# A gated delta-rule layer with a ternary feed-forward: weight sums taken in the recurrence's last chunk, GpSimd's tables moved forward

## The reference

```
q, k, v = silu(causal_conv4(x @ Wq/Wk/Wv)); a = sigmoid(x @ Wa + ba); beta = sigmoid(x @ Wb + bb)
for t in 512 steps:                       # state St: 128 x 128 per batch and head
    err = St k_t - v_t
    St  = a_t * St - (beta_t * err) k_t^T
    o_t = St q_t
x = layernorm(x + ((norm(o) * ln_w + ln_b) * sigmoid(x @ Wg)) @ Wo)
```

```
scale = mean(|W|) + 1e-8
Wq    = clip(round(W / scale), -1, 1) * scale
x     = layernorm(x + (silu(x @ Wup^T) * (x @ Wgate^T)) @ Wdown^T)
```

## Time and profile before

| | |
|---|---|
| Time, median of 3 runs | 3029.47 us (3019.24 to 3034.47) |
| The profiled execution | 3027.24 us, of it the span of the profile 3025.5 us |
| Busy in the span | PE 2701.4, DVE 2054.5, POOL 1434.1, ACT 1184.1 us |
| Stages, from the windows of the trace | projections 0 to 935, recurrence 935 to 2222, attention output 2222 to 2551, ternary 2551 to 2624.6, feed-forward 2624.6 to 3025.5 us |
| Granted clock of TensorE (share of full speed) | recurrence 0.97, ternary 0.72 |
| GB/s in the ternary stage | 171 |

### The profile page before, as it was taken

One profiled execution on the slowest core, in us unless ns is written; L12 is line 12 of the kernel. 1 busy time (PEld: TensorE's weight loads), 2 busy tenths in 40 slices (PEclk: granted clock), 3 DMA queues, 4 the chain that ended last, 5 costly groups with the idle time before them and its releaser, 6 DMA issues. The chain is left out here.

```text
span 3025.5 us, 57383 instructions
## 1 busy us (share of the span) xinstructions
PE 2701.4 (89%) x18370; PEld 2279.9 (75%) x18370; DVE 2054.5 (68%) x5896; ACT 1184.1 (39%) x2305; POOL 1434.1 (47%) x1213
## 2 busy tenths in 40 slices
...
DMA packets 412562, 442.27 MB, mean 146 GB/s; under 512 B 122304, under 2 KB 367040, under 8 KB 389568
## 3 DMA queue, kind: packets, MB, share of 16 engines
...
...
## 5 line engine op out<-in xcount | busy, mean ns | idle before, releaser
L355 PE MATMUL pa_ps<-pa_x_hi,pa_w_hi 128*128 128x512 f32 x1296 | 507.5, 392 | 10.4 <-ACT pa_y L298 6.2
L355 PE MATMUL pa_ps<-pa_x_lo,pa_w_hi 128*128 128x512 f32 x1296 | 505.1, 390 | 0.0
L355 PE MATMUL pa_ps<-pa_x_hi,pa_w_lo 128*128 128x512 f32 x1296 | 504.9, 390 | 0.0
L1030 DVE TENSOR_TENSOR pb_tmp<-pb_gb,pb_ps 128x112 f32<-128x112 f32 (+6 forms) x1792 | 328.2, 220 | 98.7 <-POOL pb_gb L721 88.6
L438 DVE SCALAR_TENSOR_TENSOR pa_cv<-pa_y,pa_taps,pa_cv 128x2048 f32<-128x2048 f32 x144 | 354.8, 2464 | 17.8
L1035 DVE TENSOR_TENSOR pb_ps<-pb_ps,pb_tmp 128x112 f32<-128x112 f32 (+6 forms) x1792 | 331.3, 226 | 6.3 <-DVE pb_tmp L1030 3.1
L721 POOL TENSOR_TENSOR pb_gb<-pb_gb,pb_ng 128x448 f32<-128x448 f32 (+6 forms) x448 | 330.9, 778 | 2.3 <-DMA pb_gb<-scratch_pairs 2.3
L904 PEld LDWEIGHTS pb_ps<-pb_Gm,pb_XT 128*128 128x128 f32 x2048 | 248.7, 196 | 68.9 <-issue 38.6
L355 PEld LDWEIGHTS pa_ps<-pa_x_hi,pa_w_hi 128*128 128x128 f32 x1296 | 243.7, 188 | 69.0 <-ACT pa_y L298 11.1
L705 POOL TENSOR_TENSOR pb_UT<-pb_UT,pb_crow 128x1024 f32<-128x1024 f32 x120 | 280.5, 2361 | 11.9 <-DMA pb_crow<-scratch_crow 11.9
L355 PEld LDWEIGHTS pa_ps<-pa_x_hi,pa_w_lo 128*128 128x128 f32 x1296 | 243.7, 188 | 50.9
...
## 6 DMA issues: line engine op xcount, KB each, us to landing
...
```

The lines of the kernel that those rows point to most:

```text
L355: last = nc.tensor.matmul(out, w[:, mat, k, :], xx[:, k, b * S:(b + 1) * S], start=(k == 0 and n == 0), stop=(k == KT - 1 and n == 2))
L1030: tt(tmp[:, hs, 0:w], gb[n][:, hs, off[t]:off[t] + w], xs[:, qs, t:t + 1].broadcast_to([P, QUART, w]), ALU.mult).then_inc(s_mul, 1)
```

## The change

In `recurrence`, GpSimd's order within a chunk is another: `with_gates(c, 1)` stands directly behind `with_gates(c, 0)`, `with_gates(c, 2)` behind the first two decays, `with_gates(c, 3)` behind the scaling of slot (1, 0); decays 4 and 5 go between the scalings of block 1 and block 2. In the last chunk, SP loads the three feed-forward matrices in 12 pieces of 1 MB into the four free 1 MB areas of `kq[0]` and `crow`, and ScalarE takes from them 48 absolute sums over 512 columns, 6 after each slot's copies, into a tile `part` that outlives the stage. In `ternary`, the sums and ScalarE's part of them are gone; all three scales are made once, at the beginning; VectorE's two passes are `w * (1/scale) + M` with M = 1.5 * 2^23 (which rounds to a whole number) and a clamp to M-1 and M+1; ScalarE's copy out of PSUM subtracts M. The weights are still loaded a second time in `ternary`.

```diff
@@ recurrence, SP
+            def feed_forward_weights():
+                sp.wait_ge(s_tp, T_START + T_CH * (NCH - 2) + T_KT[3] + 1)
+                sp.wait_ge(s_dp, D_START + D_CH * (NCH - 1))
+                sp.wait_ge(s_us, 8 * (NCH - 1))
+                for k in range(PIECES):
+                    if k >= 4:
+                        sp.wait_ge(s_fa, 4 * (k - 3))
+                    sp.dma_start(ff_stage[k % 4].rearrange("p (n d) -> p n d", n=4),
+                                 weight_piece(ff_views, k // 4, k % 4)).then_inc(s_fw[k % 4], 16)
...
             chunk(NCH - 2, 0, True, False)
+            feed_forward_weights()
             chunk(NCH - 1, 1, False, False)
@@ recurrence, GpSimd
             def chunk(c, i, p, more):
                 with_gates(c, 0)
+                with_gates(c, 1)
...
+                with_gates(c, 2)
                 less_v(c, D_START + D_CH * c, 1)
-                with_gates(c, 1)
...
                         if (n, hf) == (1, 0):
-                            with_gates(c, 2)
-                        if (n, hf) == (1, 1):
                             with_gates(c, 3)
+                        if n + hf == 2 and more:
+                            if n == 1:
+                                pool.wait_ge(s_crl, 32 * c + 32)
+                                pool.wait_ge(s_dp, D_START + D_CH * c)
+                            decay(3 + n)
                 if more:
-                    pool.wait_ge(s_crl, 32 * c + 32)
-                    pool.wait_ge(s_dp, D_START + D_CH * c)
-                    for e in range(4, 8):
+                    for e in (6, 7):
                         decay(e)
@@ recurrence, ScalarE
+            def absolute(k):
+                j = k // 4
+                if k % 4 == 0:
+                    act.wait_ge(s_fw[j % 4], 16 * (j // 4 + 1))
+                piece = ff_stage[j % 4][:, 512 * (k % 4):512 * (k % 4) + 512]
+                nc.scalar.activation(piece, piece, ACT.Abs, accum_out=part[:, k // 16, k % 16:k % 16 + 1]).then_inc(s_fa, 1)
...
                         if not more:
+                            for k in range(6 * (2 * n + hf), 6 * (2 * n + hf) + 6):
+                                absolute(k)
                             continue
@@ ternary
-                nc.scalar.activation(junk[:, :, :], w[i % 2][:, 4 * j:4 * j + 4, :], ACT.Abs,
-                                     accum_out=part[:, i, j:j + 1]).then_inc(s_abs, 1)
...
-                    nc.scalar.activation(dest(tern, i, n), ps[2 + n % 4][:, :].rearrange("p (k e) -> p k e", k=4), ACT.Copy).then_inc(s_ev, 1)
+                    nc.scalar.activation(dest(tern, i, n), ps[2 + n % 4][:, :].rearrange("p (k e) -> p k e", k=4), ACT.Identity,
+                                         bias=back[:, 0:1]).then_inc(s_ev, 1)
...
+            nc.vector.tensor_reduce(tot[:, :], part[:, :, :], AX.X, ALU.add).then_inc(s_scale, 1)
+            nc.vector.tensor_scalar(scales[:, :], ps[0][:, 0:3], 1.0 / COUNT, 1e-8, ALU.mult, ALU.add).then_inc(s_scale, 1)
+            nc.vector.reciprocal(inv[:, :], scales[:, :]).then_inc(s_scale, 1)
...
-                    nc.vector.tensor_scalar(ll, ww, half[:, i, 1:2], None, ALU.is_lt).then_inc(s_low, 1)
-                    dve.wait_ge(s_low, 4 * i + j + 1)
-                    nc.vector.scalar_tensor_tensor(out=ww, in0=ww, scalar=half[:, i, 0:1], in1=ll, op0=ALU.is_gt, op1=ALU.subtract).then_inc(s_q, 1)
+                    dve.wait_ge(s_w[i % 2][j], 16 * (i // 2 + 1))
+                    nc.vector.tensor_scalar(ww, ww, inv[:, i:i + 1], MAGIC, ALU.mult, ALU.add).then_inc(s_q, 1)
+                    dve.wait_ge(s_q, 8 * i + 2 * j + 1)
+                    nc.vector.tensor_scalar(ww, ww, MAGIC + 1.0, MAGIC - 1.0, ALU.min, ALU.max).then_inc(s_q, 1)
```

More of the change, by code:

```diff
@@ L465, in _, with weight_views, weight_piece, recurrence @@
             head(NH - 1, False, False)
-def recurrence(nc, scr):
+def weight_views(mats):
+    return [mats[0].rearrange("(n p) d -> p n d", p=P), mats[1].rearrange("(n p) d -> p n d", p=P),
+            mats[2].rearrange("(n p) (m d) -> p n m d", p=P, d=HID)]
+def weight_piece(views, i, j):
+    return views[i][:, 4 * j:4 * j + 4, :] if i < 2 else views[i][:, j, :, :]
+def recurrence(nc, scr, mats, part):
     GR = HB // 4
@@ L541, in recurrence @@
         s_os = [m.sem(f"os{i}") for i in range(2)]
+        s_fw = [m.sem(f"fw{i}") for i in range(4)]
+        s_fa = m.sem("fa")
         T_START, T_CH = 12, 32
@@ L565, in recurrence @@
         flat = lambda t: t.rearrange("p h t -> p (h t)")
+        PIECES = 12
+        ff_views = weight_views(mats)
+        ff_stage = [flat(kq[0][:, 0, :, :]), flat(kq[0][:, 1, :, :]), flat(crow[:, 0:16, :]), flat(crow[:, 16:32, :])]
         window = lambda w: (slice(16 * w, 16 * w + 16), slice(max(16 * w - BL, 0), 16 * w + BL))
@@ L649, in _ @@
             sp.wait_ge(s_te, 8 + 4)
-            sp.dma_start(scr["crow"].rearrange("c h v -> h c v"), decay_rows).then_inc(s_cw, 16)
+            sp.dma_start(scr["crow"].rearrange("c h v -> h c v"), decay_rows).then_inc(s_cr, 16)
             load_kq(1, 1)
-            sp.wait_ge(s_cw, 16)
+            sp.wait_ge(s_cr, 32)
             load_crow(0, 0)
@@ L1430, in _, with ternary @@
                 nc.vector.bn_aggr(stat[:, c, :], bn_all[:, c, :])
-def ternary(nc, mats, tern, scales):
+def ternary(nc, mats, tern, scales, part):
     NP = E * HID // P // HID
     COUNT = float(E * HID)
+    MAGIC = 1.5 * 2.0 ** 23
     with ExitStack() as ctx:
@@ L1442, in ternary @@
         w = [m.sb(f"w{i}", [P, NP, HID]) for i in range(2)]
-        junk = m.sb("junk", [P, 4, HID], mybir.dt.bfloat16)
-        low = m.sb("low", [P, 4, HID])
         ident = m.sb("ident", [P, P])
         ones = m.sb("ones", [P, P])
-        part = m.sb("part", [P, 3, 4])
+        back = m.sb("back", [P, 1])
         tot = m.sb("tot", [P, 3])
-        half = m.sb("half", [P, 3, 2])
+        inv = m.sb("inv", [P, 3])
         ps = [m.ps(f"ps{i}") for i in range(8)]
         s_id = m.sem("id")
-        s_c = m.sem("c")
         s_w = [[m.sem(f"w{i}_{j}") for j in range(4)] for i in range(2)]
-        s_abs = m.sem("abs")
-        s_tot = m.sem("tot")
-        s_sum = m.sem("sum")
-        s_sc = m.sem("sc")
-        s_low = m.sem("low")
+        s_scale = m.sem("scale")
         s_q = m.sem("q")
@@ L1477, in _ @@
             make_identity(nc, pool, ident, s_id)
-            nc.gpsimd.memset(ones[:, :], 1.0).then_inc(s_c, 1)
+            nc.gpsimd.memset(ones[:, :], 1.0).then_inc(s_id, 1)
+            nc.gpsimd.memset(back[:, :], -MAGIC).then_inc(s_id, 1)
         @block.scalar
         def _(act):
-            def absolute(i, j):
-                act.wait_ge(s_w[i % 2][j], 16 * (i // 2 + 1))
-                if i or j:
-                    act.wait_ge(s_abs, 4 * i + j)
-                nc.scalar.activation(junk[:, :, :], w[i % 2][:, 4 * j:4 * j + 4, :], ACT.Abs,
-                                     accum_out=part[:, i, j:j + 1]).then_inc(s_abs, 1)
-            for i in range(2):
-                for j in range(4):
-                    absolute(i, j)
+            act.wait_ge(s_id, 4)
             for i in range(3):
@@ L1495, in _ @@
                     act.wait_ge(s_tr, NP * i + n + 1)
[L1496 to L1498 removed]
+                    nc.scalar.activation(dest(tern, i, n), ps[2 + n % 4][:, :].rearrange("p (k e) -> p k e", k=4), ACT.Identity,
+                                         bias=back[:, 0:1]).then_inc(s_ev, 1)
         @block.tensor
         def _(pe):
[L1502 to L1503 removed]
+            pe.wait_ge(s_id, 3)
+            pe.wait_ge(s_scale, 1)
+            nc.tensor.matmul(ps[0][:, 0:3], ones[:, :], tot[:, :], start=True, stop=True).then_inc(s_scale, 1)
             for i in range(3):
[L1505 to L1506 removed]
                 for n in range(NP):
                     j = NP * i + n
[L1509 removed]
+                    pe.wait_ge(s_q, 8 * i + 2 * (n // 4) + 2)
                     if j >= 4:
```

33 lines of the change are left out of this document (8 added, 25 removed).

## The result

The changed kernel takes 3015.86 us (median of 20 runs, 3002.19 to 3026.81), the kernel before in the same rounds 3038.99 (20 runs, 3019.24 to 3056.22): ratio 0.9922, 95% interval 0.9907 to 0.9937, so 23.7 us less (19 to 28). The direction is as predicted, the time is not: 2997.0 was said, 2982 to 3010 the range. The profiled execution took 3009.76 us, its span is 3008.0: 17.5 us less than the profiled one before.

A forecast was written before the change was run, and what follows sets the result against it. The TensorE-ScalarE ring was taken to bound the recurrence, VectorE its last chunk. From 3027.24 us, -3.3 - 4.2 + 8.5 - 32.4 = -31.4 gave 2995.8, with 2.2 for the median 2998; 2997 was said, range 2982 to 3010.

The forecast's parts named there:

- Ternary, -32.4: Ternary stage: two VectorE passes a piece fit under the 2.71 us DMA, so DMA bounds it; 32.4 us less.
- Rival D: Ternary stage: VectorE's two passes run at 2.35 us each, 25 us later, 3022; chance 0.05.
- Rival B: Ternary stage: TensorE stays at the low clock throughout, 10 us later, 3007; chance 0.11.
- The 48 sums, +8.5: Last chunk: ScalarE's sums at 0.62 us delay the copies of X, +7.4, plus 1.1 for TensorE's clock.
- 1.1 for one or two such slots: Last chunk: added for eight transposes at TensorE's low clock, 0.8 us a slot.
- Rival C: Last chunk: sums cost the upper bound, +17 (0.75 us each, every slot at low clock), 3006; chance 0.10.
- Chunk 0, -4.2: Chunk 0: table 1 made before GpSimd's wait for `crow`, so slot (1, 0)'s transposes start 4.2 us earlier; bounds 0 and 11.8.
- Chunks 1 to 14, -3.3: Tables moved forward end VectorE's wait; ScalarE's key copy is late next: 0.39 us in 7 chunks, 0.08 in 7.
- The reading of the ring: Recurrence: TensorE and ScalarE (transposes, copy, products, key copies, next copy of X) bound it; VectorE's 57.2 us wait lies beside.
- rival A: Recurrence: GpSimd's tables are on the path after all, 57.2 us go instead of 3.3, 2943; chance 0.05.
- Rival E: Recurrence: decay 4 waits for `crow` ahead of block 2's scaling, 3049; chance 0.03; sign: GpSimd waiting ahead of L732.
- the level: Whole kernel: starting time, the profiled execution's 3027.24 us, with the median of the runs put 2.2 us higher.

The follow-up runs named there:

- experiment 3: Changed kernel plus matmuls that nobody reads (fillers) on TensorE ahead of the last chunk's transposes, where it waits for ScalarE's sums: ratio 0.9902 to the kernel before.
- the two second profiles: One more profiled execution each of the kernel before and the changed kernel, both unchanged: 3037.57 and 3025.64 us.
- experiment 1: Kernel before with GpSimd's new order alone, nothing else of the change: ratio 0.998 to the kernel before.
- 2: Changed kernel with GpSimd's old order, so the sums and the two-pass rounding alone: ratio 0.9956 to the kernel before.
- 9: Kernel before without the eight filler matmuls ahead of the state products at a chunk's end: ratio 0.9975, median 3025.48 us.
- 10: Kernel before with GpSimd's new order alone and without the eight filler matmuls at a chunk's end: ratio 0.9895, median 3005.15 us.
- experiment 6: Kernel before, unchanged, profiled a second time: 3037.57 us in one execution.
- 11: Kernel of 8 without more fillers, ahead of state products of heads 0 to 7 and block 3's cross products: ratio 1.0039, 3049.54 us.
- 12: Kernel of 8 with the eight filler matmuls put back at the end of chunk 14 alone: ratio 0.9784 to the kernel before.
- 5: Changed kernel with the last chunk's sums moved (5 ahead of key copies, 6 in five slots, 13 behind the last copies) and fillers there: ratio 0.9873.
- 8: Kernel of 5 without the eight filler matmuls ahead of the state products at a chunk's end: ratio 0.979, 2972.7 us.

## Why the prediction was wrong

**Ternary, -32.4: right, -31.9**, by its own steps (first piece, pieces 2.70 us apart, passes of 1.29 and 1.23 us, end). Four copies with the bias take 2.46 us (4.91 for eight) instead of 2.06. Rival D (passes of 2.35 us) is out. Rival B (half clock all through) is out as well: windows of 4 us show a clock of 0.76 at 2576 and 1.00 in all of the following. With float32 transposes alone on it TensorE gets the full clock here:
```profile
2580.00:2584.00 4.00, 3.44 (x31) 2.98 (x29) 3.77 (x4) 4.00 (x8) 0.00 (x0) 1.00 1.04 386
```
The Trainium skill ("TensorE: Matmul & The Clock Gate", "Part 4: PE-mode transpose") says that transposes don't count as busy in the same way and don't bring the full clock. This trace doesn't agree, with 1.00 in every window from 2580 on.

**The 48 sums, +8.5: the step that failed**, by the size of one term, TensorE's clock. The part on ScalarE was right: the sum at 0.61 us, 6.5 in all instead of 7.4 (experiment 3). The clock was put at "1.1 for one or two such slots". It came to 7.0, of which 14.45 - 10.34 = 4.1 in the step to slot (1, 0), and 0.5 more in the tail. 6.5 + 7.0 + 0.5 = 14.0. The prediction had read eight transposes at the low clock, 0.8 us, and no more. It left out that in block 0 the cross products (3.52 instead of 2.00 us) and the key products (3.43 instead of 2.00) stand between two copies of X as well, and that the price is paid just where the new pause is longest. Rival C was half of this. Its low clock in slot after slot came (in three of the steps and in the long first one), its other half, sums of 0.75 us, did not; +17 was its bound, 14.0 the result.

**Chunk 0, -4.2: right in kind, -5.5 to chunk 1** (-3.6 between the two second profiles, where the clock stood low for longer in the changed one). The transposes of slot (1, 0) start at 996.74 behind GpSimd's scaling; by the forecast 997.4, with the stage 2.2 us earlier.

**Chunks 1 to 14, -3.3: right at the same clock; what the clock does there was put at nothing.** Over the three profiles with the old order and the six with the new one, all with the original fillers there, a chunk of chunks 2 to 13 takes on average:

| | old order | new order |
|---|---|---|
| odd chunk, no fall | 76.74 | 76.57 |
| even chunk, no fall | 78.66 | 78.38 |
| even chunk, fall of 3.4 us | 80.12 | 79.62 |

So the order is worth 0.45 to 0.67 us a pair, 3.1 to 4.7 us in the seven pairs. The reading of the ring was right: of 57.2 us of waits the path had next to nothing, and rival A is out. The rest of the difference in the profiles is falls. Short ones (3.4 or 6.8 us, 1.2 to 1.5 us of time for each 3.4) stand in 12 of 14 even chunks without a long fall in the old order and in 15 of 31 in the new, which is why a pair is 1.4 to 2.3 us shorter in the changed profile than in that of before. Long ones cost some 9 us each; there are three in the changed profile against one, and they turn -3.3 into +8.7. Rival E's first sign came: GpSimd waits for `crow` ahead of decay 4 in all of chunks 1 to 14 but one, 0.2 to 1.7 us, where the prediction had a cover of 2.8 us or more.
```profile
1252.40 2.36 POOL L732 TENSOR_TENSOR pb_UT<-pb_UT,pb_crow 128x1024 f32<-128x1024 f32 x1 [1.61 <-DMA pb_crow<-scratch_crow]
```
Its price did not come, since TensorE never waits for GpSimd's scaling in chunks 1 to 14. As timed over many executions, the order in all is worth 6 us (experiment 1), 10 us (2 against the changed kernel), and 20 to 24 us without the eight fillers (9, 10), where the clock is higher with it as well.

**The sum.** Part by part against kernels without it: ternary -31.9, the sums 78.8 - 62.8 = +16.0 (GpSimd's order alone had made the last chunk 2.0 shorter), the order -6.1 as timed: -22.0 us, measured -23.7 (-28 to -19). And the level: the forecast started from the profile's 3027.24 us, the kernel before has a median of 3038.99 over 20 runs. Of the 18.9 us by which the time was missed, 31.4 - 23.7 = 7.7 are the change's, the rest is that level. The profile before was one of the quicker executions: one long fall, where a second profile (experiment 6) had two and took 3037.57 us. So the second step that failed is the first term of the sum, the level: "the median of the runs is 2.2 higher" came from three runs, and over 20 it is 11.8 higher. This is the larger part of the miss; either error alone would have left the time inside the range.

**What stays open.** Why long falls come. In chunks 1 to 14 the three profiles with GpSimd's old order (and the original fillers) have 1, 1 and 2, the six with the new one 3, 4, 4, 2, 3 and 3. That is 4 in 42 chunks against 19 in 84, suggestive and no more, since they move from execution to execution, and the mean granted clocks of all executions (0.9585 and 0.958 in experiment 1) don't bear it out. They have a fixed place: each of the 23 begins 2.1 to 2.7 us behind its chunk's first `less_v`, in even chunks in the old order (4 of 4) and mostly in odd ones in the new (14 of 19). A busy stretch without a gap isn't enough to bring them (11). Missing fillers brought them to every chunk in one kernel (11), but putting fillers back did not remove the one in the last chunk (12). No kernel here was run that tells the phase of the chunk apart from its contents.

## What to carry over

Work put on an idle engine costs what it delays on the critical ring, and then once more what the pause does to TensorE's clock: price every product between two steps of the ring at both clocks, not only the next one. Look for the places where that engine itself waits for TensorE (here ahead of the key copies), and fill those first: the same 48 sums cost 12 to 16 us (78.8 and 75.2 against 62.8) or 1.7. And when single profiles are compared, count the falls of the clock in each before reading a difference of 10 us as the change's: compare chunks of the same clock, and take the level of the forecast from many runs.

## What the runs showed of the chip

- A fully busy TensorE can lose its clock. It fell to 0.50 for 20.5 us within stretches without a gap; a chunk of 76.6 us then takes 85.9. Over the 20 runs of the changed kernel the time follows the mean granted clock: 3002.19 us at 0.964, 3026.81 at 0.954.
- Fillers work both ways: eight bf16 products of 512 columns more or less in a chunk changed the kernel by 25 us (5 and 8; in GpSimd's old order only by 8, with no gain inside the interval, 9), and another eight by some 75 in the other direction (8 and 11).
- An activation with an accumulator read follows another at 0.61 us for 128x512 (2178.43 to 2179.04), against 0.52 for a plain copy; the next activation starts 0.09 us behind the start of the read, which takes 0.19.
- A two-operation pass of VectorE over 128x2048 float32 takes 1.23 us with constants and 1.29 with one operand per partition.
